# Attention and mixture of experts on one core: values of seven groups with the head dimension on the partitions

## The reference

```
xn = layernorm(x)
q, k, v = xn @ Wq.T, xn @ Wk.T, xn @ Wv.T           # 8 heads of 32
# blocks of 12 queries, each sees 24 keys: its own block and the one before
logits = q_block . k_ctx + rel_shift(q_block . rel_k)
logits = tanh(logits / 50) * 50
attn   = softmax(logits, axis=-1)
out    = attn @ v_ctx                                # per head, 32 wide
x = x + out @ Wpost.T + moe(xn)                      # 8 experts of 704, top 2, silu(gate) * up
```

## Time and profile before

| | |
|---|---|
| median of 3 runs | 769.17 us (768.98 to 770.46) |
| the profiled execution | 771.75 us |
| its span in the trace | 770.0 us |
| PE busy | 745.6 us, 97% |
| PEld busy | 688.0 us, 89% |
| DVE busy | 466.4 us, 61% |
| ACT busy | 359.7 us, 47% |
| POOL busy | 352.9 us, 46% |
| mean granted PE clock | 0.992 of full speed |

### The profile page before, as it was taken

How to read it: one execution, slowest core, us unless ns; L and a number is a source line. 1 busy time by engine, 2 the same in 40 slices (tenths; PEclk the granted TensorE clock), 3 DMA queues, 4 the chain that set the end, 5 groups by cost and what they waited for, 6 DMA issues and landing times.

```text
span 770.0 us, 19528 instructions
## 1 busy us (share of the span) xinstructions
PE 745.6 (97%) x6487; PEld 688.0 (89%) x6487; DVE 466.4 (61%) x1212; ACT 359.7 (47%) x654; POOL 352.9 (46%) x262
## 2 busy tenths in 40 slices
PE   6999999999999999999999999999999999999993
PEld 5898999999999998899999999999999999999992
DVE  3465368788799975555555555555555555555551
ACT  4667777667666576333333333333333333333330
POOL 3465566666664547133333444434433333344422
PEclk9999999999999999999999999999999999999997
DMA  8543689999998772122473562563463662222221
GB/s 251 155 156 91 186 274 329 313 316 321 307 305 272 199 131 59 40 36 36 100 189 70 143 171 43 129 157 67 108 180 65 154 158 42 41 43 43 40 29 20
DMA packets 66455, 111.07 MB, mean 144 GB/s; under 512 B 15561, under 2 KB 48921, under 8 KB 66361
## 3 DMA queue, kind: packets, MB, share of 16 engines
q0 software_dynamic: 19216, 43.31, 23.7%
q1 hardware_dynamic: 31073, 41.96, 18.8%
q10 hardware_dynamic: 16072, 24.51, 10.0%
HBM read 66.89 MB, written 42.88 MB: 143 GB/s over the span
## 4 chain that ended last, share of the span: by engine, by line
PE 86%; DVE 7%; DMA 3%; issue 2%; ACT 1%; POOL 0%; SPq 0%; ACTq 0%; POOLq 0%; DVEq 0%
PE psum L1417 79%; PE psum L1547 4%; DVE spare_m L1201 3%; DMA bd_d<-arena 1%; PE psum L1505 1%; DMA out<-spare,sca_i 1%; DVE spare_m L1203 1%; PE psum L1432 1%; DVE xg_m L1203 1%; DMA x_all<-in_x 1%; DMA arena<-bd_d 1%; PE psum L1632 1%; PE psum L1623 0%; DVE arena L1353 0%; DVE arena L1297 0%
## 5 line engine op out<-in xcount | busy, mean ns | idle before, releaser
L1417 PE MATMUL psum<-w_ring,xT 128*128 x1206 | 281.1, 379 | 0.5 <-DVE xT L1241 0.5
L1417 PEld LDWEIGHTS psum<-w_ring,xT 128*128 128x128 f32 x1206 | 214.0, 188 | 29.3 <-issue 0.6
L659 POOL DMA_INDIRECT xg<-xn_d,gat_i x67 | 70.2, 1047 | 238.6 <-DVE spare L1403 212.0
L1417 PE MATMUL psum<-w_ring,hT 128*128 x1139 | 152.0, 287 | 1.5 <-DVE spare L1403 1.1
L849 ACT ACTIVATE xT<-psum,nwp 128x128 fp32r<-128x128 f32 x134 | 41.9, 364 | 216.7 <-PE psum L1505 183.1
L1417 PEld LDWEIGHTS psum<-w_ring,hT 128*128 128x128 f32 x1139 | 140.3, 191 | 1.8 <-issue 1.8
L732 POOL DMA_INDIRECT out<-spare,sca_i x67 | 106.7, 1592 | 41.3 <-issue 19.4
L1241 DVE SCALAR_TENSOR_TENSOR xT<-psum,nwp,xT 128x128 fp32r<-128x128 f32 x134 | 40.9, 347 | 135.1 <-ACT xT L849 133.0
L703 POOL TENSOR_TENSOR arena<-arena,const 120x540 f32<-120x540 f32 x38 | 51.0, 1343 | 106.9 <-DVE arena L1287 103.5
L1227 DVE SCALAR_TENSOR_TENSOR spare<-psum,slot_w,spare 128x704 f32<-128x704 f32 x67 | 63.7, 951 | 43.3 <-PE psum L1417 27.0
L1417 PE MATMUL psum<-arena 32*120 32x108 f32 (+1 forms) x1216 | 85.5, 262 | 0.0
(11 more groups left out here) (186 smaller groups left out, 985.4 us busy)
## 6 DMA issues: line engine op xcount, KB each, us to landing
w_split<-w_ring POOLq DMA_DIRECT2D x20, 1088.0 KB, 7.9
w_ring<-w_split SPq DMA_DIRECT2D x40, 544.0 KB
raw<-in_w_raw ACTq DMA_DIRECT2D x20, 544.0 KB, 6.8
w_ring<-in_w_raw ACTq DMA_DIRECT2D x12, 544.0 KB, 5.8
arena<-in_x SPq DMA_DIRECT2D x37, 108.0 KB
out<-arena SPq DMA_DIRECT2D x37, 108.0 KB
arena<-xn_d SPq DMA_DIRECT2D x31, 120.0 KB
x_all<-in_x ACTq DMA_DIRECT2D x2, 1024.0 KB, 7.2
```

Of the source, the lines that this page charges most:

```text
L659: pool.indirect_dma_start(out=xg[:, b % NXG, :], out_offset=None, in_=xn_d, in_offset=bass.IndirectOffsetOnAxis(ap=gat_i[:, b:b + 1], axis=0),
L1417: return pe.matmul(out_ap, lhs, rhs, start=first, stop=last)
```

## The change

For groups 0 to 6 (`N_COL` = S_PC - 3 = 7, the steps 4 to 10) the values are computed the other way round. v of one head (120 keys by 32) is stationary and the exponentials (120 by 108) move, so that the result has the head dimension on 32 partitions and the queries along the free dimension; four heads lie on the four strips of 32 partitions. A second set of products has a 120 by 32 block of ones as the stationary operand and gives the denominators, repeated on all 32 partitions. `inverted` takes the reciprocal of all 216 denominators per partition; `divided_early` multiplies and writes back into PSUM, over the denominators, in natural order of the blocks (two instructions, odd and even blocks). The logits' copy stands between the two. No transpose is needed, and the rounding reads the divided values from PSUM. All products of a group now wait for POOL's mask. Groups 7 and on are computed as before; their waits count from where they begin. The first 12 columns of oT_hi and oT_lo, which the early groups do not write, are zeroed once by POOL.

```diff
@@ buffers, semaphores, helpers
+        rden_all = sb("rden_all", [P, KD, GQ])
+        s_zero = sem("s_zero")
+        N_COL = S_PC - 3
+        o_ps = psum[:, 6, 0:KD * GQ].rearrange("p (k n) -> p k n", k=KD)
+        o_sums = psum[:, 6, KD * GQ:2 * KD * GQ].rearrange("p (k n) -> p k n", k=KD)
+        def by_block(rows):
+            return rows.rearrange("p k (n c) -> p k n c", c=CHUNK)
+        def divisions(g):
+            return g + 1 + min(g + 1, N_COL)
@@ pool
             pool.memset(o_sb[:, :, :], 0.0).then_inc(s_ini, 1)
+            pool.memset(oT_hi[:, :, 0:PAST].bitcast(F32), 0.0).then_inc(s_zero, 1)
+            pool.memset(oT_lo[:, :, 0:PAST].bitcast(F32), 0.0).then_inc(s_zero, 1)
@@ vector
+            def inverted(g):
+                dve.wait_ge(s_pv, g + 1)
+                dve.reciprocal(rden_all[:, :, :], o_sums).then_inc(s_rc, 1)
+            def divided_early(g):
+                dve.wait_ge(s_rc, g + 1)
+                for blocks, first in ((slice(0, NODD), 1), (slice(NODD, GB), 0)):
+                    dve.tensor_tensor(by_block(o_sums)[:, :, first::2, :], by_block(o_ps)[:, :, blocks, :],
+                                      by_block(rden_all)[:, :, blocks, :], ALU.mult).then_inc(s_o, 1)
@@ divided
-                if g:
-                    dve.wait_ge(s_ot, g)
+                if g > N_COL:
+                    dve.wait_ge(s_ot, g - N_COL)
@@ split_out
-                dve.wait_ge(s_ot, g + 1)
+                if g < N_COL:
+                    dve.wait_ge(s_o, divisions(g))
+                else:
+                    dve.wait_ge(s_ot, g + 1 - N_COL)
                 if g:
                     dve.wait_ge(s_po, g)
+                else:
+                    dve.wait_ge(s_zero, 2)
+                if g < N_COL:
+                    rows, o = slice(PAST, GK), o_sums
+                else:
+                    rows, o = slice(0, GK), psum[:, 6, 0:KD * GK].rearrange("p (k n) -> p k n", k=KD)
-                dve.tensor_copy(oT_hi[:, :, :], o_ps).then_inc(s_oth, 1)
+                dve.tensor_copy(oT_hi[:, :, rows], o).then_inc(s_oth, 1)
                 dve.wait_ge(s_oth, g + 1)
-                dve.tensor_tensor(oT_lo[:, :, :], o_ps, oT_hi[:, :, :].bitcast(F32), ALU.subtract).then_inc(s_ote, 1)
+                dve.tensor_tensor(oT_lo[:, :, rows], o, oT_hi[:, :, rows].bitcast(F32), ALU.subtract).then_inc(s_ote, 1)
@@ the loop on vector
-                if s >= 4:
+                if 4 <= s < N_COL + 4:
+                    inverted(s - 4)
+                if s >= N_COL + 4:
                     divided(s - 4)
                 if 0 <= s - S_L - 1 < TT // TPS:
                     tile_logits(s - S_L - 1)
+                if 4 <= s < N_COL + 4:
+                    divided_early(s - 4)
@@ values, on tensor
+                if g < N_COL:
+                    pe.wait_ge(s_mk, g + 1)
+                    for k in range(KD):
+                        for i in range(HC):
+                            r = slice(DH * i, DH * (i + 1))
+                            mm(psum[r, 6, k * GQ:(k + 1) * GQ], v1[0:GK, g % 5, HC * k + i, 0:DH],
+                               ex[0:GK, g % 2, KD * i + k, :], True, True)
+                    for k in range(KD):
+                        for i in range(HC):
+                            r = slice(DH * i, DH * (i + 1))
+                            ins = mm(psum[r, 6, (KD + k) * GQ:(KD + k + 1) * GQ], ones[0:GK, 0:DH],
+                                     ex[0:GK, g % 2, KD * i + k, :], True, True)
+                    ins.then_inc(s_pv, 1)
+                    return
@@ turn_out
-                pe.wait_ge(s_o, g + 1)
+                pe.wait_ge(s_o, divisions(g))
```

More of the change, by code:

```diff
@@ L1300, in split_out @@
             def split_out(g):
-                dve.wait_ge(s_ot, g + 1)
+                if g < N_COL:
+                    dve.wait_ge(s_o, divisions(g))
+                else:
+                    dve.wait_ge(s_ot, g + 1 - N_COL)
                 if g:
                     dve.wait_ge(s_po, g)
-                o_ps = psum[:, 6, 0:KD * GK].rearrange("p (k n) -> p k n", k=KD)
-                dve.tensor_copy(oT_hi[:, :, :], o_ps).then_inc(s_oth, 1)
+                else:
[5 more added lines that the diff above has]
+                dve.tensor_copy(oT_hi[:, :, rows], o).then_inc(s_oth, 1)
                 dve.wait_ge(s_oth, g + 1)
-                dve.tensor_tensor(oT_lo[:, :, :], o_ps, oT_hi[:, :, :].bitcast(F32), ALU.subtract).then_inc(s_ote, 1)
+                dve.tensor_tensor(oT_lo[:, :, rows], o, oT_hi[:, :, rows].bitcast(F32), ALU.subtract).then_inc(s_ote, 1)
             def split_piece(n):
```

## The result

| | before | after |
|---|---|---|
| median | 770.26 us (20 runs, 768.85 to 778.66) | 767.72 us (20 runs, 766.19 to 770.56) |
| ratio after to before | | 0.9959 (95%: 0.9942 to 0.9976) |
| the profiled execution | 771.75 us, span 770.0 | 770.56 us, span 768.8 |

What follows compares the result with a forecast made beforehand. PE was taken as the bound, hanging on DVE's queue in each changed step. Six steps at 0.12 + 0.19 (1.9 us) plus 0.6 in step 6 took 2.5 off 769.17: 766.7 us, range 765.5 to 768.0 (for all, 764.3 to 769.4).

Steps and rivals of the forecast that it cites:

- The place: In the seven changed steps PE hangs on DVE's queue: the logits' copy releases PE and would wait for the reciprocal.
- Values: Strip products on PE in steps 4 to 10: 0.11 us a round of four, values 0.66 us shorter by themselves.
- rival C: Strip products on PE: weight loads exposed when strips hold different weights, 0.22 us a round, slower at 772.2 us; chance 0.10.
- Reciprocal: DVE's reciprocal of 216 elements per partition, ahead of the logits' copy: 1.50 us, bounds some 0.4 and 1.87.
- Rival B: DVE's reciprocal costs its upper bound, 1.87 us, so the turn of rows comes 0.25 late; 769.0 us, chance 0.15.
- D: DVE's reciprocal streams at about 1 ns an element, the copy waits for the turned logits again; 763.5 us, chance 0.07.
- The turn of rows: PE's turn after the logits' copy: at V+2.81 instead of V+2.93, so 0.12 of the 0.66 us saved arrives.
- old V: Start of the values in a loop step of the kernel before, 85.71 in step 9; forecast times count from it.
- Step 6: Held by ScalarE's table load and square root, which release DVE; gain 0.6 us instead of 0.31.
- The transposes: Two output transposes between queries and keys, on PE's path behind its wait: removing them gains 0.19 us a step.
- What is late next: DVE's longer chain behind the copy: output ready at about V+5.2, `project` at V+5.81, so 0.6 us of cover.
- Rival E: The gain is given back where DMA queues run at 0.84 of their time; 769.2 us, chance 0.08.

Runs made afterwards that it cites:

- e2_div_first: Changed kernel with DVE dividing before it copies the logits; median 771.96 us, ratio 0.9998 to the kernel before, V to V 8.63 us in step 9.
- e3_split_recip: Changed kernel with the reciprocal cut in two, 144 elements before the logits' copy and 72 behind it; median 767.18 us, ratio 0.9942 to the kernel before.
- e5_short_recip: Changed kernel with the reciprocal taking only 8 of 216 denominators, for timing only; one execution 770.44 us, steps 8 and 9 of 7.74 and 7.75 us.

## Why the prediction was right

**The place.** The forecast said that PE would be released by the copy of the logits, and the copy by the reciprocal. It is so in the after profile, and `e2_div_first`, `e3_split_recip` and `e5_short_recip` move the step by changing nothing but that.

**Values.** Forecast: 0.11 a round, v rows 0.66 earlier. Measured: 0.093 a round, and from the logits' start to the v rows 83.86 - 82.55 = 1.31 us instead of 87.25 - 85.14 = 2.11, 0.80 less. That is the bound I gave for rounds in proportion to the columns (108 against 128); I had taken the logits' round unscaled, and it was mis-sized by 0.14. The strips hold the v of four different heads and run side by side all the same, so rival C is out. The Trainium skill's rule that a weight load overlaps running products only when its row group differs ("TensorE: Matmul & The Clock Gate", section "The mechanism") does not hold for these strips either: all rows are in use, and 16 loads of 0.11 us and 16 products pass in 0.37 us. The same section also has loads pulled ahead when they go to the background weight buffer, which the prediction left out; no run shows whether that is what happens here.

**Reciprocal.** Forecast 1.50 us from the 8- and 32-element rows, measured a mean of 1507 ns over seven:

```profile
L1294 DVE RECIPROCAL rden_all<-psum 128x216 f32<-128x216 f32 x7 | 10.6, 1507 | 11.4 <-PE psum L1463 11.4
```

Rival B (1.87) and D are out, and so is the repeat count of 8 in the Trainium skill's page "VectorE: DVE Perf Modes", section "First, the fixed hardware budget", taken as cycles per element: with the page's 0.96 GHz that is an estimate of 8.3 ns; the page itself gives no time. From 72 elements (0.60) to 216 (1.51) it is 6.3 ns. What I left out is that the copy starts 0.08 before the reciprocal ends and takes 0.13 there instead of 0.19, together 0.14 us less.

**The turn of rows and the sum.** Counted from the old V (0.57 behind the start of the logits), the turn of rows comes at 85.70 - 82.55 - 0.57 = V+2.58, where I had V+2.81: 0.1 because the shorter rounds let the reciprocal start at V+0.88 instead of V+0.98, 0.14 from the copy. So 0.52 arrive instead of 0.31 in steps 8 and 9. In steps 4, 5, 7 and 10 it is less, 0.40 to 0.45 from V to V: step 4 waits for ScalarE instead, and behind step 10 the values are full width again and follow the logits by 0.57, not 0.46. Step 6 shortened from 9.48 to 8.78, 0.70 instead of 0.6, and DVE was released there by ScalarE, as said. 2 x 0.52 + 4 x 0.44 + 0.70 gives the 3.5 us of the stage, against my 2.5.

**The transposes.** 0.19 forecast, 0.17 measured by putting them back (in steps 8 and 9).

**What is late next.** `project` starts at 88.73 and its input is ready at 87.74; the forecast had 0.6 us of cover, it is 1.0. Counted from the old V, the input is ready at V+4.62 instead of V+5.2: 0.23 because the copy ends earlier, 0.11 in the divisions (0.46 together), the rest in the mask, `rest_v` and the rounding; `project` itself comes 0.2 earlier. POOL's mask and the memsets cost nothing, as said.

**The whole.** 3.5 us in the stage became 2.5 and 3.3 us between the medians of the two comparisons (3.2 and 2.9 us by their ratios, 0.41 and 0.37%). Rival E, that the gain is given back, was right in part and wrong in its reason: not the DMA queues' load, but an end that is 1 to 1.5 us longer, and now and then a stretch at the lower clock. That the total came so near to the forecast is in part luck: the stage gave 1.0 us more than forecast, and the end, which the forecast left as it was, took 1 to 1.5 us back.

## What to carry over

When PE's work ahead of a wait is shortened, ask what the wait's releaser does in between: here, in steps 8 and 9, each of three things (products, reciprocal, the copy's position in DVE's queue) moved the step, the reciprocal until the turned logits became the limit, though PE stood idle next to all of them. A long operation that a short, urgent one must not wait for can be cut in two around it. And a cover that hides a longer chain belongs to a step, not to the kernel: one step further, without the turns of rows, the same edit (with the split reciprocal) gained 0.14 us, where it gained 0.86 in each of steps 8 and 9.

## What the runs showed of the hardware

- Products with 32 stationary columns, outputs in four strips of 32 partitions: 108 moving fp32 columns (120 rows) take 0.093 us for a round of four PE instructions, with v of four heads in the strips as with the same ones in all four; 128 columns (128 rows, the logits) take 0.11 to 0.13. A change from strips to full width costs 0.11 to 0.12 us more than strips behind strips (0.57 against 0.46 behind the logits).
- DVE's reciprocal in fp32 takes 6.2 to 6.4 ns for each further element per partition, from 8 elements (0.20 us) to 216 (0.60 us for 72, 1.06 for 144, 1.51 for 216), and 8 elements from PSUM take as long as from SBUF (0.203 and 0.204).
- DVE's copy of the logits, which needs nothing of the reciprocal in front of it, starts 0.08 us before that ends.
- DVE writes to PSUM about as fast as to SBUF: two products of 96 and 120 elements per partition with source and result in PSUM take 0.46 us together, one of 256 from PSUM to SBUF 0.42.
- A 16 KB piece of the instruction queue that ends 0.7 to 1.6 us later goes with a scatter that lands 0.7 to 1.5 us later; the scatter behind it starts 1.9 to 2.0 us after the piece's end in all thirteen profiles.
- Profiles of one kernel differ by 1.6 us in the first 20 us alone, with the granted clock (0.83 or 1.00 between 10 and 20 us), while steps 8 and 9 repeat to 0.03 us. A comparison by stage sees what the medians can't.
